# A strip-mined two-layer vision kernel: halo rows kept on chip, sums on GpSimd, and work moved out of a strip's tail

## The reference, cut to what matters

```
x = x + conv0(ln_c(x))         # per pixel, over the 96 channels
t = t + ffn0(ln_t(t))          # t: x as tokens; 96 -> 384 -> 96, fp8/fp16 rounding
x = x + conv1(ln_c(x))
t = t + ffn1(ln_t(t))

conv0: qkv = qkv_w @ x + b; windows of 8x8 queries, each with the 12x12 keys and
       values around it (2 pixels of padding), 6 heads of 16;
       softmax(q k + relative position) v; projection
conv1: feat, value = 1x1 convolutions; the image is folded 2x2; in each quarter and
       head 4 centres = feat pooled over a quarter of it;
       sim = sigmoid(beta + alpha * cos(centre, point)); each point keeps its best;
       agg = (sum of sim * value + pooled value) / (sum of sim + 1);
       out = agg of the point's centre * sim; projection
```

## Time and profile before

| | us |
|---|---|
| median of 3 runs | 9565.71 (9555.72 to 9568.57) |
| profiled execution | 9573.13 |
| its span, first to last instruction | 9571.3 |
| PE busy | 8344.2 (87%) |
| DVE busy | 7322.2 (77%) |
| ACT busy | 4988.4 (52%) |
| POOL busy | 2176.8 (23%) |
| mean granted clock of TensorE | 0.905 |

### The profile page before, as it was taken

One profiled execution on the slowest core, in us unless ns is written; L12 is line 12 of the kernel. 1 busy time (PEld: TensorE's weight loads), 2 busy tenths in 40 slices (PEclk: granted clock), 3 DMA queues, 4 the chain that ended last, 5 costly groups with the idle time before them and its releaser, 6 DMA issues.

```text
span 9571.3 us, 441216 instructions
## 1 busy us (share of the span) xinstructions
PE 8344.2 (87%) x175538; PEld 6638.7 (69%) x175538; DVE 7322.2 (77%) x24166; ACT 4988.4 (52%) x9994; POOL 2176.8 (23%) x4356
## 2 busy tenths in 40 slices
PE   8999999998888888888888888988888989888665
PEld 6777777777767767777777766776777777776443
DVE  5777777778787777787777778777778778877666
ACT  3555445445555555555555555555555555555445
POOL 2323222222222222222222222222222222222000
PEclk9999999999999999999999999999999999998555
DMA  2111112112122122222222212222222222221111
GB/s 59 49 45 46 49 49 52 50 47 60 53 58 59 53 56 59 55 58 57 55 54 59 56 51 58 58 55 54 60 55 55 60 55 54 60 55 50 57 57 61
DMA packets 191968, 525.03 MB, mean 55 GB/s; under 512 B 33372, under 2 KB 66972, under 8 KB 189980
## 3 DMA queue, kind: packets, MB, share of 16 engines
q1 hardware_dynamic: 190204, 498.89, 19.3%
HBM read 252.61 MB, written 168.30 MB: 44 GB/s over the span
## 4 chain that ended last, share of the span: by engine, by line
PE 59%; DVE 26%; issue 8%; ACT 6%; DVEq 1%; SPq 0%; ACTq 0%; DMA 0%; POOL 0%; POOLq 0%
PE scores_x L644 10%; PE flipped L666 6%; PE bank L551 5%; PE misc L560 4%; PE pv L694 3%; PE bank L614 3%; PE bank L912 3%; DVE maxes L1510 3%; PE pv L688 3%; PE scores_x L585 2%; DVE z L1625 2%; PE bank L939 2%; PE pv L895 2%; PE bank L621 2%; DVE shifted L1518 2%
## 5 line engine op out<-in xcount | busy, mean ns | idle before, releaser
L1510 DVE TENSOR_REDUCE maxes<-scores_x 128x6 f32<-128x864 f32 x1024 | 1079.1, 1054 | 1046.3 <-PE scores_x L644 973.6
L1957 POOL TENSOR_TENSOR vrest<-vstage,vmask 96x384 f32<-96x384 f32 x512 | 431.5, 843 | 5592.6 <-ACT vstage L1141 5592.6
L644 PE MATMUL scores_x<-keys,queries 64*64 64x144 f32 x24576 | 1101.4, 313 | 436.6 <-DVE shifted L1518 414.8
L644 PEld LDWEIGHTS scores_x<-keys,queries 64*64 64x64 f32 x24576 | 803.8, 144 | 678.0 <-issue 627.9
L1179 ACT ACTIVATE probs<-flipped 128x384 f32<-128x384 f32 x1024 | 497.6, 486 | 1320.1 <-PE flipped L666 1320.1
L1518 DVE TENSOR_TENSOR shifted<-scores_x,maxes 128x768 f32<-128x768 f32 x1024 | 970.2, 948 | 0.0
L606 PE MATMUL bank<-xn,wq 97*32 97x64 f32 x24576 | 869.4, 221 | 56.7 <-issue 56.0
L666 PE MATMUL flipped<-ident,shifted 128*128 128x128 f32 x6144 | 918.6, 289 | 0.1
L603 PE MATMUL bank<-xt,wq 97*32 97x64 f32 x24576 | 846.6, 221 | 65.3 <-issue 51.0
L603 PEld LDWEIGHTS bank<-xt,wq 97*32 97x32 f32 x24576 | 727.7, 110 | 248.7 <-issue 224.8
L1129 ACT ACTIVATE queries<-bank 128x512 f32<-128x512 f32 x768 | 458.6, 597 | 835.6 <-PE bank L606 835.6
(11 more groups left out here) (185 smaller groups left out, 18387.2 us busy)
## 6 DMA issues: line engine op xcount, KB each, us to landing
x_in<-x_dram SPq DMA_DIRECT2D x128, 594.0 KB
keys<-kst SPq DMA_DIRECT2D x768, 99.0 KB
xn_kept<-xn SPq DMA_DIRECT2D x128, 388.0 KB, 3.9
later<-xn_kept SPq DMA_DIRECT2D x128, 388.0 KB, 3.3
x_tok<-tok_dram SPq DMA_DIRECT2D x128, 384.0 KB, 3.5
x_kept<-x SPq DMA_DIRECT2D x128, 384.0 KB, 2.4
later<-x_kept SPq DMA_DIRECT2D x128, 384.0 KB, 3.7
out_dram<-later SPq DMA_DIRECT2D x128, 384.0 KB, 2.5
```

The lines of the kernel that those rows point to most:

```text
L644: last = mm(score[e][64 * j:64 * j + 64, g * NKEY:(g + 1) * NKEY], queries[64 * e:64 * e + 64, g, w, :], keys[64 * e:64 * e + 64, g, :, WS ...
L1510: V.tensor_reduce(maxes[:, p % 2, :, :], sc, AX.X, ALU.max).then_inc(max_ready.sem, 1)
```

## The change

- Kept rows. A strip prepares only its 8 new rows, 1056 columns, in three chunks of 352. The 4 rows above come from the strip before: GpSimd copies the last 528 columns of `xn` and of `kst` to the front (`keep_halo`). The quarters are now walked down the columns, so that 32 strips in a row continue each other; at the four starts of a column the rows come from HBM (`load_top`, `take_top`), where they are put at the beginning by two extra strips, -2 and -1 (`store_tops`).
- The first values of strip n+1 leave the tail of n: `make_values(n, 0)` stands where `make_values(n, 1)` stood, and that goes behind scores(1).
- Mixing leaves the tail: PE's `mix` stands behind `pool` at p = 5, VectorE's behind `normalise(0)` at p = 5, and PE's spread at p = 6 waits for it.
- `next_stats` goes from the tail to p = 6, `pool_stats` to p = 7.
- The second half of the FFN's statistics and normalisation goes from the tail to p = 0 and 1 of the next strip, `flip_z(n-1, 1)` from p = 0 to p = 2. The root of the second FFN joins that root (`with_c`), and the root of x's variances joins that of the features' lengths (columns 32 to 43 of `rs_b_chain`).
- All variances of x stand at p = 3. GpSimd adds the tokens of xn2 in two additions, and `pool` has one matmul for each half.

```
 PE, attend
                 scores(0)
                 if b1: flip_z(n - 1, 0)
-                make_values(n, 1, work)
+                make_values(n, 0, work)
                 for p in range(TILES): scores(p + 1)
+                    if p == 0:
+                        if on.c3: pe.wait_ge(hc_evac.sem, hc_evac.at(n - 1, 6))
+                        make_values(n, 1, fill)
...
                     if p == 3 and ahead:
-                        variance(n + 1, 2, on)
-                        variance(n + 1, 3, on)
+                        for c in range(3): variance(n + 1, c, on)
...
                     if p == 6:
+                        if on.c1:
+                            pe.wait_ge(mixed.sem, mixed.at(n, 2))
                         if ahead: spread(n + 1, 0); spread(n + 1, 1)
...
-                    if p == 2 and ahead: ... variance(n + 1, 0, on); variance(n + 1, 1, on)
+                    if p == 2 and b1:
+                        if on.b: pe.wait_ge(ft_ready.sem, ft_ready.at(n, 2))
+                        flip_z(n - 1, 1)
...
                     if p == 5:
                         if b2: pool(n - 2)
+                        if on.c1:
+                            pe.wait_ge(v_stored.sem, v_stored.at(n, 8))
+                            mix(n, 0)
+                            mix(n, 1)
 PE, tail
-                if on.c1: for u in range(2): ... mix(n, u)
-                    make_main(n + 1, 0, fill)
-                    make_rest(n + 1, 0, fill)
 PE, pool
+                pe.wait_ge(xn2_summed.sem, xn2_summed.at(n, 2))
                 for u in range(2):
-                    for j in range(4): mm(..., xn2[:, 4 * u + j, :], pool_w, ...)
+                    mm(..., xn2_sum[:, u, :], pool_w, start=True, stop=True)
 DVE, attend
+                    if p == 0: ... if b1: ffn_stats(n - 1, 1)
+                    if p == 1 and b1: ffn_normalise(n - 1, 1, False, on.c2)
                     if p == 5:
                         ... second_order(rs_b_chain, ..., finals, at)
                         if on.b: cosine(n)
                         normalise(0)
+                        if on.c1: mix(n, 0, par); mix(n, 1, par)
                     if p == 6: ... output(n - 1, 0); output(n - 1, 1)
+                            next_stats(n - 1)
                     if p == 7: ... residual(0); hidden_c(n, 2); hidden_c(n, 3)
+                        if b1: pool_stats(n - 1)
-                if on.c1: mix(n, 0, par); mix(n, 1, par)
-                if b1: next_stats(n - 1)
                 normalise(1)
                 ffn_stats(n, 0)
-                if b1: pool_stats(n - 1)
                 ffn_normalise(n, 0, b1)
...
                 residual(1)
-                ffn_stats(n, 1)
-                ffn_normalise(n, 1, False)
 DVE, drain
                     mix(n, 0, par); mix(n, 1, par)
                 if on.b:
+                    lone_root(n)
                     cosine(n)
 POOL
+            def keep_halo(n):
+                pool.wait_ge(q_ready.sem, q_ready.at(n, 6))
+                pool.wait_ge(win_ready.sem, win_ready.at(n, 4))
+                P.tensor_copy(xn_flat[0:PROW, 0:TOP], xn_flat[0:PROW, NEW:STRIP]).then_inc(halo_ready.sem, 1)
+                pool.wait_ge(k_loaded, n * (16 * NH) + 16 * NH)
+                P.tensor_copy(kst[0:C, 0:TOP], kst[0:C, NEW:STRIP]).then_inc(halo_ready.sem, 1)
 POOL, strip
                 mask_values(n, 0)
                 repeat_rest(n, 2)
+                if column: take_top(column)
+                elif on.ahead: keep_halo(n)
                 if on.b2: normalise_stream(n - 2)   # now with two additions behind it
 SP
+            def store_tops(u):      # for strips -2 and -1
+                sp.dma_start(top_xn[u, :, :], xn_new[0:PROW, :])
+                sp.dma_start(top_keys[u, :, :], kst[0:C, TOP:STRIP])
+            def load_top(j):        # at the start of column j
+                sp.dma_start(xn_flat[0:PROW, 0:TOP], top_xn[j // 2, :, at:at + TOP])
+                sp.dma_start(kst[0:C, 0:TOP], top_keys[j // 2, :, at:at + TOP])
```

More of the change, by code:

```diff
@@ L81, in stage, with build @@
               x2=n + 2 < N, reused=n > LAG_B)
[L84 removed]
+def build(nc, x, tok, consts, out, x2_kept, xn2_kept, sims_kept, top_xn, top_keys):
     with ExitStack() as ctx:
@@ L451, in store_out, with strip @@
                              ).then_inc(out_stored, 16)
-            def strip(n, par, on):
+            def strip(n, par, on, column=0):
+                if column:
+                    load_top(column)
                 load_residual(n)
@@ L748, in attend @@
                     if p == 3 and ahead:
-                        variance(n + 1, 2, on)
-                        variance(n + 1, 3, on)
+                        for c in range(3):
+                            variance(n + 1, c, on)
                     if p == 4:
@@ L825, in attend @@
                 weigh(TILES - 1)
-                if on.c1:
-                    for u in range(2):
-                        if ahead:
-                            pe.wait_ge(normed.sem, normed.at(n + 1, 4 - u))
-                        pe.wait_ge(v_stored.sem, v_stored.at(n, 8))
-                        mix(n, u)
                 if ahead:
@@ L1067, in _ @@
             setup()
-            for c in range(4):
-                mean(0, c)
-            for c in range(4):
-                variance(0, c)
-            for c in range(4):
-                spread(0, c)
-            for c in range(4):
-                make_keys(0, c)
+            for n in (-2, -1, 0):
+                if n > -2:
+                    pe.wait_ge(k_stored.sem, k_stored.at(n, 0))
+                for c in range(3):
+                    mean(n, c)
+                for c in range(3):
+                    variance(n, c)
+                for c in range(3):
+                    spread(n, c)
+                for c in range(3):
+                    make_keys(n, c)
             for i in range(6):
                 make_queries(0, i)
-            make_values(0, 0, fill)
             for n in range(2):
@@ L1540, in attend @@
                             normalise_c(n, 1 - par)
+                    if not ahead and p == 4 and on.b:
+                        lengths(n)
                     if ahead and p == 4:
@@ L1990, in _ @@
             strip(2, stage(2))
-            with pool.Fori(3, N - 1) as n:
-                strip(n, stage(3))
+            for j in range(1, STARTS + 1):
+                with pool.Fori(max((j - 1) * COLUMN, 3), j * COLUMN - 1) as n:
+                    strip(n, stage(3))
+                if j < STARTS:
+                    strip(j * COLUMN - 1, stage(3), j)
             strip(N - 1, stage(N - 1))
@@ L2099 @@
                                 ("sims_kept", TILES * SW))]
+    kept += [nc.dram_tensor(name, (2, rows, NEW), F32, kind="Internal").ap()
+             for name, rows in (("top_xn", PROW), ("top_keys", C))]
     build(nc, x_ap, tok_ap, aps, o_ap, *kept)
```

344 lines of the change are left out of this document (218 added, 126 removed).

## The result

The changed kernel takes 9828 us (median of four runs, 9808 to 9855) against 9567 (four runs of before, 9556 to 9582): ratio 1.0274, 95% interval 1.0242 to 1.0305. It is 2.7% slower. The forecast was 9310, faster.

The account below looks back on a forecast made before the run. It took the fixed order of nearly full TensorE and VectorE as the bound. Gains of 216 (C), 66 (B) and 59 (A), less 60, 10 and 20, made 251 us, from 9571.3 to 9320, given as 9310; range 9100 to 9540.

Parts of the forecast that it names:

- Head, C: Scores(0) to scores(1) in the last stage (C, everything on, 94 strips): 3.4 us, the 4.1 us stall becoming 0.4.
- Mixing at p=5: Scores(6) to scores(7) in C: VectorE's additions hold the maximum, TensorE stands 2.5 us, step 9.15 us against 6.05.
- Rival (3): GpSimd's new work holds VectorE at p=1 and p=6: 1.5 us a strip, 9450 us, chance 0.14.
- So the tail is VectorE's now: End of a C strip: gather waits for VectorE's simw, scores(0) 9.75 us after the last weighing, TensorE waiting 0.9.
- The cover named as the next to fail: Tail: the keys' transfers land 11.7 us after the first keys began, just when scores(0) stand ready.
- the clock's cost: Low clock level in a C strip: 4.1 us of cost, 5.1 before, bounds 1 and 9.
- the sum that it is added to: A C strip's eight steps and loop at the high clock: 65.4 us, 66.7 before.
- The rival called slower: Mixing's stall brings the low level where TensorE sets the pace: C from 72.2 us, 74 giving 9730; chance 0.11.
- A and B: First stage (first layer only, 18 strips) gains 3.3 us a strip, middle stage (features added, 16 strips) 4.1.
- Third spread: At p=7 TensorE's third spread waits for VectorE's normalise_x(0): 1.8 us of new stall in C, 1.5 in A.
- Start: Two extra strips and slow 97-row stores before strip 0: first maximum near 138 us instead of 77.11, 60 lost.
- Kept rows: Means, variances, spreads, keys on fewer columns, with fewer pooling passes: 4.9 us less TensorE work a strip, 4.3 at high clock.

Follow-up runs that it names:

- mix_tail: The changed kernel with the mixing back in the strip's tail on both engines: 9343 us, ratio 0.975 to the kernel before.
- before_mix: The kernel before with the mixing alone moved to p=5, as in the change: 9728 us, ratio 1.0175.
- mix_late: The changed kernel with VectorE's two mixing additions behind p=6's maximum, TensorE's order untouched: 9665 us, ratio 1.0078 to the kernel before.
- late_dense: mix_late plus two unused identity products of the mixing's size behind the last weighing: 9727 us, ratio 1.0161 to the kernel before.
- val_tail: The changed kernel with only the first values' products back in the tail among the queries: 9722 us, ratio 1.0157 to the kernel before.
- mix_val: The changed kernel with the mixing and the first values both back in the tail: 9292 us, ratio 0.9717 to the kernel before.
- fill: The changed kernel with unused identity products ahead of scores(3), scores(7) and the third spread: 9742 us, ratio 1.0204 to the kernel before.
- mix_fill: mix_tail plus unused identity products ahead of scores(3) and the third spread: 9511 us, ratio 0.9938 to the kernel before.

## Why the prediction was wrong

**Head, C: right.** The step is 4.4 us, 1.1 of it at the low clock, for 3.4 forecast; the 4.1 us stall is gone.

**Mixing at p=5: the step right, its worth wrong.** Forecast 9.15 with a wait of 2.5; measured 8.98 with 2.52. The price was taken as 3.1 us against the 6.05 of before; with the mixing in the tail the step is 5.02, so it is 4.0. Rival (3), GpSimd holding VectorE, is not seen at this place: the two additions took 1.08 us together, before 1.10. The step of the prediction that failed is the next one, the tail that the mixing, the first values and a fourth of the keys leave. The prediction paid 3.1 us at scores(7) and took more than that back in the tail, which it put at 21.3 us for 25.3 before. The runs show that the tail gets nothing from the mixing's leaving: 23.4 us with it, 25.0 without. Two parts of that can be read. In C, leaving out the strips at the starts of quarters, tails with under 0.3 us of low clock take 23.0 us in the changed kernel (only 7 of 76), 23.5 in mix_tail (58) and 25.2 before (69). So at the high clock the whole change takes about 2 us from the tail and not 4, and the mixing's leaving 0.5. The rest is low clock, 4.7 us a tail. The runs tie it to the mixing's place (0.4 in mix_tail; 3.3 in before_mix for 0.0 before) but not to the wait at scores(7) (mix_late has none there, and 6.4 in the tail). Products in the old place lower it to 2.4 and leave the tail as long as it was (late_dense). Why it comes stays open.

**"So the tail is VectorE's now": wrong.** PE, VectorE and the wait in a tail without low clock behind the last weighing of the changed kernel:

```profile
7106.52 0.60 PE L753 MATMUL pv<-vmain,probs 128*32 128x17 f32 x48
...
7117.61 0.54 PE L972 MATMUL pv<-later,simw 128*32 128x97 f32 x16
7118.68 0.97 PE L703 MATMUL scores_x<-keys,queries 64*64 64x144 f32 x24 [0.53 <-ACT queries L1187]
```

```profile
7116.37 0.29 DVE L1807 TENSOR_TENSOR simw<-winners,sims 128x128 f32<-128x128 f32 x1 [0.24 <-DVE winners L1802]
```

```profile
PE bank L665 <- issue: 1.4, 1, 1.4
```

And VectorE's wait for gather in the C window:

```profile
DVE sums_em L1813 <- PE pv L972: 32.7, 13, 3.7
```

VectorE has simw 9.5 us behind the weighing, near the forecast 9.1, but gather starts at 10.5: PE's own queries took that long, where the working had 8.7. It is so in the other strips too: in the C window no gather waits for simw, and VectorE waits for gather in all 13. Of the strip shown, 1.4 us is a gap in which PE waits for nothing that the profile shows; such gaps among the queries are 26.5 us in 13 strips (14.3 + 12.2). Before, in the window of the earlier trace rows, they are 11.7:

```profile
PE bank L606 <- issue: 6.9, 7, 1.6
...
PE bank L603 <- issue: 4.8, 5, 1.1
```

Then scores(0) wait for the last queries' store, not for the keys. The cover named as the next to fail, the keys' transfers, held. What left the tail was taken off a sum that had none of these gaps, 2.0 us a strip now. It is the values' leaving that brings them: val_tail puts nothing but the values back and has 9.2 us of them, and with the mixing in the tail the same edit takes them from 20.8 (mix_tail) to 9.0 (mix_val). What PE lacks in a gap is not shown.

**C: the clock's cost right, the sum that it is added to wrong.** A line was laid through the strips of C, length against time at the low level, with the strips at quarter starts left out (76 strips). It gives 67.6 us + 0.36 for each us at the low level after, and 63.6 + 0.38 for mix_tail; by pairs of strips, which takes out VectorE's loop turn, 67.9 + 0.35 and 64.1 + 0.34. So after the change the high-clock sum is near 68 where the prediction had 65.4, and the low level costs some 4.5 us for the forecast 4.1: the error is in the sum. The tail has 2 us of it, and the rest is spread over the other steps. Before, the line depends on the strips taken, 65.8 + 0.56 and by pairs 67.7 + 0.37, so the prediction's 66.7 and its half of the low time are neither confirmed nor refuted. About 4 of the mixing's 5 us are in the high-clock sum and 1 in the clock (13.6 us of low clock a strip for 10.1). The rival called slower, "mixing's stall brings the low level", with 74 us a strip and 9730, was the nearest to what came; what it lacked was A, and its cause, the stall, is not what the runs bear out.

**A and B: wrong, and most of it is clock.** The prediction took 4.3 us of work off A and put the clock at nothing there, without a reason. The line for A gives 54.3 us at the high clock before and 54.6 + 0.43 a us after: at the high clock nothing was won or lost, and the 17.9 us of a strip at the low level (before 1.3) are the 7.3 us. In B, where 4.1 us were forecast, 1.3 came, and the low level rose from 7.9 to 10.0 us a strip. A strip's head in A with the low level, and one without, then the clock over the same stretches:

```profile
1040.06 1.72 PE L703 MATMUL scores_x<-keys,queries 64*64 64x144 f32 x24 [0.81 <-ACT queries L1187]
...
1045.33 1.72 PE L703 MATMUL scores_x<-keys,queries 64*64 64x144 f32 x24
...
859.62 0.97 PE L703 MATMUL scores_x<-keys,queries 64*64 64x144 f32 x24 [0.79 <-ACT queries L1187]
863.00 0.96 PE L703 MATMUL scores_x<-keys,queries 64*64 64x144 f32 x24 [0.16 <-DVE shifted L1578]
```

```profile
1039.50:1044.80 5.30, 4.74 (x42) 4.39 (x43) 2.83 (x7) 1.50 (x3) 0.00 (x0) 0.50 0.02 3
859.00:862.40 3.40, 2.72 (x41) 2.39 (x42) 1.72 (x3) 1.27 (x3) 0.00 (x0) 1.00 0.00 0
```

From scores(0) to scores(1) it is 5.27 us in the one and 3.38 in the other, with the same work and no wait of note. The stage table shows what brings it. Over the 18 strips of A, a strip takes 56.6 us with the FFN half and the values in the tail, 58.9 and 59.1 with the values in the head, 61.0 and 61.3 with the FFN half there, and 61.3 to 62.4 with both (before 55.3). So these two moves are 4.7 of the 6.0 us, the FFN half alone between 2.4 and 4.7: it makes VectorE late at scores(3), 31.1 us in 13 strips against 3.0. The forecast had 0.3 us for that FFN root, and only in C; in A the same root stands in a strip whose steps are 3.4 to 5 us long. Products in PE's idle time take off little, 60.5 and 60.8 us (fill, mix_fill) against 61.3 to 62.4. With FFN half and values back, A still has 8.7 us at the low level a strip, and its third spread still waits 19.5 us in 13 strips, 2.0 before; `next_stats`, which stands ahead of it at p=6 in every kernel here, was not put back. Why the clock is low there is open; the split variances did not tell.

**Third spread.** 1.8 forecast in C, 10.2 us in 13 strips measured, 0.8. As I read it, PE comes to it later, since scores(7) and all behind them are late; in mix_late, where scores(7) are not, it is 1.7. In A, where 1.5 was forecast, it is 1.5.

**Start.** First maximum at 126.29, 49 us later than before; forecast 138, though the terms listed for it (two stores of 20.5, two strips' work of 9, the top's 10) make 69 and not 61. The stores' term held: VectorE waits 18.3 us for each of the two 97-row stores (36.7 together), 400 KB in some 18 us, 22 GB/s.

```profile
69.38 0.95 DVE L1527 TENSOR_TENSOR xn<-x_in,bank 97x352 f32<-97x352 f32 x2 [18.34 <-DMA top_xn<-xn]
...
126.29 1.06 DVE L1570 TENSOR_REDUCE maxes<-scores_x 128x6 f32<-128x864 f32 x1 [18.34 <-PE scores_x L703]
```

**Kept rows.** Most of the 4.3 us of PE work in C is there: with mixing, FFN half and values put back the strip is 3.6 us shorter than before.

## What to carry to other kernels

In an engine with a fixed order, an instruction that waits for another engine is priced by what stands behind it, not by its own length: two additions of 0.5 us held a ready maximum for 5.6 us. A move out of a full stretch pays only for as long as the stretch has no second bound close behind; write down the measured length of a stretch beside the sum of its parts (here 2 us of gaps were in no part) before anything is subtracted. And a change of several parts is read part by part, in more than one order: all but the mixing were worth 2.5% together, the mixing cost 5.2%, and the FFN half was worth 176 us of C beside one place of the mixing and 19 beside the other.

## What the runs showed of the hardware

The granted clock is a term of its own, and a stage that has none of the low level can get it from a change that takes work away: A went from 0.99 to 0.86 while PE's busy time stretched from 683.5 us to 714.6 for less work. A microsecond at the low level went with 0.43 us of length in A, where PE sets the pace, and with 0.34 to 0.38 in C after the change and in mix_tail. It does not follow idle time simply. Behind the 2.52 us wait the clock was 0.62, yet putting eight products into that wait did not change the time clear of noise (9856 against 9828). And with products put in the tail (late_dense against mix_late) the tail's low time fell from 6.4 to 2.4 us while that of the next head's first two steps rose from 2.7 to 11.0.
